# Adding the maximum of a unit's first score buffer directly behind its scores, ahead of the previous unit's last weighted sums

## The chip, the cores and the metric

The kernel is one program on one core of a Trainium2 chip. The metric is the device time of one execution in microseconds (us), the median of several runs; less is better. Work is spread over five engines that each run their own instruction stream and meet at semaphores: TensorE (PE, with its weight loads shown apart as PEld), VectorE (DVE), ScalarE (ACT), GpSimd (POOL), and SyncE (SP), which issues most DMAs.

## The reference

One pre-norm transformer block on 2048 tokens of width 128: an attention layer with 16 heads of 64, and a feed-forward layer whose inputs and weights are rounded to a 4-bit grid in blocks of 16.

```python
qkv = layernorm(x) @ w_qkv                       # 128 -> 3 x 1024
q, k, v = split(qkv), 16 heads of 64
sim = einsum('bhid,bhjd->bhij', q, k) * 64**-0.5
attn = softmax(sim, axis=-1)
x = x + einsum('bhij,bhjd->bhid', attn, v) @ w_out + b_out
xn = layernorm(x)
gate, y = fp4_linear(xn, w_gate), fp4_linear(xn, w_up)   # both sides quantised
x = x + fp4_linear(silu(gate) * y, w_down)
```

Everything is float32. The change touches only the attention: the scores, and the row maximum that the softmax takes off them before the exponential.

## The kernel before, in words

Attention is done in 32 units: 8 pairs of heads, and for each pair 4 blocks of 512 queries. A unit goes through the 2048 keys in 16 steps `j` of 128 keys. The scores stand with keys on the 128 partitions and queries along the free axis, for two heads at a time, in one of two PSUM buffers (`s_ps`, buffer `j % 2`).

On PE, step `j` of a unit (`body`, L1174) issues, in this order:

- for even `j`, one piece of row maxima for the next unit (`row_maxima`, L1155: two matmuls into `mx_ps`, L1016 and L1023; ACT takes the positive part, `rise`, L534, and DVE adds and reduces, L790);
- the scores of step `j + 1` (`scores`, L1000: three products of high and low parts, for two heads, six matmuls), which wait until the exponential has emptied that buffer;
- for odd `j`, the piece of row maxima instead;
- in some steps one piece of other work (`misc`: projections of K, Q, V for coming units, the denominator, the output projection);
- for odd `j`, the weighted sums of steps `j - 1` and `j` (`weighted`, L1151: `probs` times V into `o_ps`), which wait for the exponentials of those steps.

The last step of a unit, `j = 15`, already computes the scores of step 0 of the next unit, into buffer 0.

The maximum itself enters as a matmul too. DVE reduces the pieces to `neg_max` (L798, at step 12), SP copies it by two small DMAs into one row per head, `mrow` (L385), and `maximum` (L1004, matmuls L1008) multiplies a column of ones with that row and adds it to the scores in PSUM. This is done only for the first two steps of a unit (`BACK = 2`). In the remaining steps the keys and values carry what is needed, so `scores` ends the group itself. The exponential of a step (ACT, L614) waits for `s_ready`, which for step 0 is raised by `maximum(0)` and for step 1 by `maximum(1)`.

In the kernel before, `maximum(0)` is the first thing of the unit that it belongs to (L1180 to L1183), so it stands behind the last weighted sums, 14 and 15, of the unit before.

ACT runs in order: exponential of step `j`, at `j = 0` also the copy of the finished `o_ps` of the unit before (`copy_output`, L536 to L540, which waits for all 16 weighted sums of that unit), then the `rise` of one piece of row maxima. POOL adds the exponentials of steps 0 to 12 for the denominator (L497), DVE those of steps 13 to 15 (L913, L918), and POOL adds the two (L503). An exponential also waits until the add that reads its `probs` buffer, four steps back, is done.

The first 24 units run as three turns of a hardware loop of 8 units (L1204); the last 8 are written out, and in them DVE, ACT and POOL already do parts of the feed-forward layer.

Of the kernel before, what the change touches and what calls it, by code (L numbers as in the profile page):

```python
# [51 lines left out]
MAX_LAND = 32  # L52
# [66 lines left out]
def misc_at(w, last):  # L119

    uses = {j: name for j, name in MISC_AT.items() if not skipped(name, w, last)}
    if last:
        uses |= WEIGHTS_AT.get(w, {})
    return dict(sorted(uses.items()))
# [10 lines left out]
def misc_before(it, w, last):  # L135

    return it * (BODY * len(MISC_AT)) + sum(len(misc_at(v, last)) for v in range(w))
# [8 lines left out]
def block_kernel(nc, x_in, w_qkv, w_out, b_out, w_gate, w_up, w_down, out):  # L146
    ctx = ExitStack()
    with ctx:
# [3 lines left out]
        def sem(name):  # L152
            return ctx.enter_context(nc.semaphore(name))
# [110 lines left out]
        s_ready = sem("s_ready")  # L264
# [14 lines left out]
        mrow_landed = sem("mrow_landed")  # L279
# [23 lines left out]
        def at(it, per_unit, w, plus=0):  # L303

            return it * (BODY * per_unit) + (w * per_unit + plus)

        def after(it, per_unit, w, plus=0):

            return at(it, per_unit, w, plus) + START

        def par(w):

            return (w // CHUNKS) % 2
# [203 lines left out]
        def _(act):  # L517
# [79 lines left out]
            def weights_t(name):  # L597

                if name == "down":
                    for i, (_, rows) in enumerate(FF_TILES):  # L600
                        ins = act.activation(wd_t[0:rows, i, :], misc_ps[0:rows, i * DIM:(i + 1) * DIM], ACT.Copy)
                else:
                    at0 = 0 if name == "gate" else FF
                    ins = act.activation(wgu_t[:, at0:at0 + FF], misc_ps[:, 0:FF], ACT.Copy)
                ins.then_inc(misc_free, 1)
# [48 lines left out]
            for what, n in ACT_ORDER:  # L654
                if what == "sign":
                    signs(n)
                elif what == "abs":
                    sizes(n)
                elif what == "T":
                    act.wait_ge(f_xt, n + 1)  # L660
                    act.activation(xq_t[:, n * NX:(n + 1) * NX], banks[4], ACT.Copy).then_inc(f_xt_copied, 1)
                elif what == "silu":
                    act.wait_ge(f_gu, n + 1)
                    if n >= 2:
                        act.wait_ge(f_h, n - 1)
                    act.activation(silu[:, n % 2, :], banks[2 * (n % 2)][:, 0:FF], ACT.Silu).then_inc(f_silu, 1)
                else:
                    act.wait_ge(f_ht, n + 1)
                    if n >= 2:
                        act.wait_ge(f_down, n - 1)  # L670
                    for i, (_, rows) in enumerate(FF_TILES):
                        ins = act.activation(hq_t[0:rows, n % 2, i, :],
                                             banks[5 + n % 2][0:rows, i * P:(i + 1) * P], ACT.Copy)
                    ins.then_inc(f_ht_copied, 1)
# [292 lines left out]
        def _(pe):  # L967
# [25 lines left out]
            def scores(buf, i, q, j):  # L993

                keys = slice(j * P, (j + 1) * P)
                parts = [(k_hi[i][:, keys], q_hi[q]), (k_hi[i][:, keys], q_lo[q]), (k_lo[i][:, keys], q_hi[q])]
                for n, (stationary, moving) in enumerate(parts):
                    for h in range(2):
                        rows = slice(DH * h, DH * (h + 1))
                        ins = pe.matmul(s_ps[:, buf, h, :], stationary[rows, :], moving[rows, :],  # L1000
                                        start=(n == 0 and j < BACK), stop=(n == 2 and j >= BACK), skip_group_check=True)
                return ins

            def maximum(buf):  # L1004

                for h in range(2):
                    rows = slice(DH * h, DH * (h + 1))
                    ins = pe.matmul(s_ps[:, buf, h, :].rearrange("p (t q) -> p t q", t=TQ), ones_r[rows, :],  # L1008
                                    mrow[rows, :].rearrange("p (q t) -> p t q", t=TQ), start=False, stop=True,
                                    skip_group_check=True)  # L1010
                return ins
# [86 lines left out]
            pe.wait_ge(pro_v, CHUNKS)  # L1098
            pe.wait_ge(pro_lo, len(PRO_LO))
            scores(0, 0, 0, 0)  # L1100

            pe.sem_inc(pv_done, P_BUFS)

# [41 lines left out]
            def weighted(it, w, j):  # L1145

                pe.wait_ge(p_ready, after(it, STEPS, w, j + 1))
                if j == 0:
                    pe.wait_ge(o_copied, at(it, 1, w, 1))
                for h in range(2):  # L1150
                    ins = pe.matmul(o_ps[DH * h:DH * (h + 1), :], vv[par(w)][:, j, DH * h:DH * (h + 1)],  # L1151
                                    probs[:, j % P_BUFS, h, :], start=(j == 0), stop=(j == STEPS - 1))
                ins.then_inc(pv_done, 1)

            def row_maxima(it, w, last, j):  # L1155

                u, s = ahead_of(w, j)
                if not runs(last, u, s):
                    return
                final = last and u == BODY  # L1160
                pe.wait_ge(mx_rise, max_no(it, w, j))
                pe.wait_ge(mx_free, max_no(it, w, j))
                if s == 0 and not final:

                    pe.wait_ge(misc_free, misc_no(it, w, "Q", last) + START + 1)
                if s == MAX_STEPS // 2 and w % CHUNKS == CHUNKS - 1 and not skipped("K", w, last):

                    pe.wait_ge(misc_free, misc_no(it, w, "K", last) + START + 1)
                if s == MAX_STEPS // 2 + 1 and w % CHUNKS == CHUNKS - 1 and not skipped("raw", w, last):

                    pe.wait_ge(misc_free, misc_no(it, w, "raw", last) + START + 1)
                max_step(s, par(u), u % Q_BUFS, par(u - 1), (u - 1) % Q_BUFS, final=final)

            def body(it, last):  # L1174
                for w in range(BODY):
                    ahead = not (last and w == BODY - 1)

                    pe.wait_ge(misc_free, misc_before(it, w, last) + START)
                    for j in range(STEPS):
                        if j == 0:  # L1180

                            pe.wait_ge(mrow_landed, at(it, MAX_LAND, w, MAX_LAND))
                            maximum(0).then_inc(s_ready, 1)  # L1183
                        if j % 2 == 0:
                            row_maxima(it, w, last, j)
                        if j < STEPS - 1:
                            pe.wait_ge(p_ready, after(it, STEPS, w, j))
                            ins = scores((j + 1) % 2, par(w), w % Q_BUFS, j + 1)
                            if j + 1 < BACK:
                                ins = maximum(j + 1)  # L1190
                            ins.then_inc(s_ready, 1)
                        elif ahead:
                            pe.wait_ge(p_ready, after(it, STEPS, w, j))
                            scores(0, par(w + 1), (w + 1) % Q_BUFS, 0)
                        if j % 2:
                            row_maxima(it, w, last, j)
                        if j in misc_at(w, last):
                            misc(misc_at(w, last)[j], it, w, last)
                        if j % 2:

                            weighted(it, w, j - 1)
                            weighted(it, w, j)

            with pe.Fori(0, ITERS - 1) as it:  # L1204
                body(it, False)
            body(ITERS - 1, True)
            misc("den", ITERS - 1, BODY, True)

# [68 lines left out]
```

## Time and profile before

| what | value |
|---|---|
| median of 3 runs | 1384.71 us (1379.86, 1384.71, 1384.8) |
| the profiled execution, its own time | 1384.4 us |
| its span, first to last instruction | 1381.5 us |
| mean granted TensorE clock | 0.978 of full |
| PE busy | 1299.0 us (94%) |
| PE weight loads busy | 674.4 us (49%) |
| POOL busy | 1053.9 us (76%) |
| ACT busy | 897.7 us (65%) |
| DVE busy | 798.2 us (58%) |

The span runs from the first to the last instruction; the execution's own time lies 2.9 us above it. Busy time on PE counts overlapping matmuls once, and the ends of matmuls are modelled: the distance from the start of one matmul to the start of the next says more about how PE advances than the duration in the row does. In a row, `x2` behind a matmul means two instructions merged, here the two heads that run side by side. What stands in brackets is the idle time of that engine in front of the instruction and what ended it; "issue" means that the profile shows nothing that the engine waited for.

### The profile page before, as it was taken

The numbers are of one execution on the slowest core, as the hardware profiler recorded it, in microseconds if no ns is written. First come the engines' busy times: TensorE is split into PE (matmuls) and PEld (weight loads), VectorE is DVE, ScalarE is ACT, GpSimd is POOL, SyncE is SP. The second block draws the span as 40 slices with busy tenths as digits, with TensorE's granted clock in tenths as the row PEclk, the third lists the DMA queues.
The fourth block names the chain that finished last, engine by engine and source line by source line (L and its number), as shares of the span: only waits on it lengthen the run. The fifth ranks groups of instructions, "written<-read, shape, count | busy, mean of one in ns | idle before, by whom it ended". The sixth has DMA issues, their size and how long they took to land.

```text
span 1381.5 us, 24376 instructions
## 1 busy us (share of the span) xinstructions
PE 1299.0 (94%) x7541; PEld 674.4 (49%) x7541; DVE 798.2 (58%) x2142; ACT 897.7 (65%) x1300; POOL 1053.9 (76%) x457
## 2 busy tenths in 40 slices
PE   4999999999999999999999999999999999898466
PEld 3555555555455555555445555555555454343245
DVE  6655555555455555555555555555555556777694
ACT  4767666677666766677666676667767667554242
POOL 4488878898778878888788888888988888789232
PEclk9999999999999999999999999999999999999787
DMA  2000000000000000000000000000000000000001
GB/s 61 2 9 2 1 2 9 2 1 1 3 9 2 2 1 9 2 1 1 3 9 2 2 1 9 2 2 1 3 1 1 1 2 1 2 1 1 1 1 30
DMA packets 18300, 6.63 MB, mean 5 GB/s; under 512 B 9696, under 2 KB 18016, under 8 KB 18160
## 3 DMA queue, kind: packets, MB, share of 16 engines
q1 hardware_dynamic: 17936, 4.40, 1.4%
q8 instruction: 66, 1.08, 0.3%
q14 instruction: 74, 0.61, 0.2%
q0 software_dynamic: 224, 0.54, 0.1%
HBM read 3.75 MB, written 1.05 MB: 3 GB/s over the span
## 4 chain that ended last, share of the span: by engine, by line
PE 85%; DVE 7%; issue 4%; POOL 2%; ACT 0%; DMA 0%; POOLq 0%; SPq 0%; DVEq 0%; ACTq 0%
PE o_ps L1151 32%; PE s_ps L1000 24%; PE mx_ps L1023 7%; PE mx_ps L1016 5%; PE misc_ps L1141 3%; PE s_ps L1008 2%; PE misc_ps L1133 2%; PE misc_ps L971 2%; PE misc_ps L983 1%; PE misc_ps L972 1%; PE misc_ps L973 1%; POOL acc_pool L497 1%; PE misc_ps L984 1%; PE misc_ps L985 1%; PE s_ps L1243 1%
## 5 line engine op out<-in xcount | busy, mean ns | idle before, releaser
L497 POOL TENSOR_TENSOR acc_pool<-acc_pool,probs 128x1024 f32<-128x1024 f32 x352 | 853.4, 2424 | 49.5 <-POOL acc_pool L497 40.3
L614 ACT ACTIVATE probs<-s_ps 128x1024 f32<-128x1024 f32 x512 | 527.3, 1030 | 122.1 <-PE s_ps L1008 67.3
L790 DVE CUSTOM_DVE_ANT_0 summed<-mx_ps,rise 128x512 bf16<-128x512 f32 x503 | 344.8, 686 | 424.9 <-issue 354.5
L1151 PE MATMUL o_ps<-probs,vv 128*64 128x512 f32 x2048 | 498.5, 607 | 5.1 <-ACT probs L614 5.1
L534 ACT ACTIVATE rise<-mx_ps 128x512 f32<-128x512 f32 x503 | 301.2, 599 | 271.7 <-PE mx_ps L1016 261.1
L1151 PEld LDWEIGHTS o_ps<-probs,vv 128*64 128x64 f32 x2048 | 127.2, 136 | 229.5 <-issue 174.8
L1016 PE MATMUL mx_ps<-k_raw,q_hi 64*128 64x512 f32 x503 | 224.5, 446 | 10.5 <-DVE part_max L790 9.2
L1023 PE MATMUL mx_ps<-k_hi,q_hi 64*128 64x512 f32 x503 | 224.5, 446 | 1.9 <-DVE part_max L790 1.8
L1000 PE MATMUL s_ps<-q_hi,k_hi 64*128 64x512 f32 x1024 | 207.0, 399 | 0.9 <-ACT probs L614 0.8
L1000 PE MATMUL s_ps<-q_hi,k_lo 64*128 64x512 f32 x1024 | 202.6, 390 | 0.0
L1000 PE MATMUL s_ps<-q_lo,k_hi 64*128 64x512 f32 x1024 | 202.4, 390 | 0.0
L503 POOL TENSOR_TENSOR acc_pool<-acc_pool,acc_dve 128x1024 f32<-128x1024 f32 x32 | 76.2, 2382 | 137.5 <-DVE acc_dve L918 137.5
L1023 PEld LDWEIGHTS mx_ps<-k_hi,q_hi 64*128 64x128 f32 x503 | 92.7, 184 | 179.0 <-issue 178.3
L806 DVE RECIPROCAL rden<-misc_ps 128x128 f32<-128x128 f32 x132 | 120.9, 938 | 13.9 <-PE misc_ps L1133 13.7
L497 POOL TENSOR_TENSOR acc_pool<-probs 128x1024 f32<-128x1024 f32 x32 | 75.9, 2370 | 61.3 <-ACT probs L614 61.3
L1000 PEld LDWEIGHTS s_ps<-q_hi,k_hi 64*128 64x128 f32 x1024 | 98.0, 187 | 38.3 <-ACT probs L614 16.6
L1016 PEld LDWEIGHTS mx_ps<-k_raw,q_hi 64*128 64x128 f32 x503 | 92.7, 184 | 34.7 <-ACT rise L534 15.2
L1000 PEld LDWEIGHTS s_ps<-q_lo,k_hi 64*128 64x128 f32 x1024 | 97.6, 186 | 21.5 <-issue 0.7
L1000 PEld LDWEIGHTS s_ps<-q_hi,k_lo 64*128 64x128 f32 x1024 | 97.0, 185 | 22.4
L814 DVE TENSOR_TENSOR o_norm<-o_raw,rden 128x512 f32<-128x512 f32 x33 | 60.5, 1834 | 0.1
L1008 PE MATMUL s_ps<-mrow,ones_r 64*128 64x512 f32 x128 | 42.6, 661 | 5.4 <-issue 5.4
L777 DVE TENSOR_TENSOR k_lo<-misc_ps,k_hi 128x512 fp32r<-128x512 f32 x28 | 19.4, 692 | 45.5 <-ACT k_hi L520 45.5
(161 smaller groups left out, 1119.0 us busy)
## 6 DMA issues: line engine op xcount, KB each, us to landing
wqkv<-in_L_attn_w_qkv SPq DMA_DIRECT2D x8, 192.0 KB, 3.3
y<-in_L_attn_x SPq DMA_DIRECT2D x4, 256.0 KB, 4.6
mrow<-neg_max SPq DMA_DIRECT2D x64, 2.0 KB, 2.0
out<-y SPq DMA_DIRECT2D x4, 256.0 KB, 2.3
wo<-in_L_attn_w_out SPq DMA_DIRECT2D x8, 64.0 KB, 1.9
wx<-in_L_ffn_w_down POOLq DMA_DIRECT2D x1, 176.0 KB, 6.6
wx<-in_L_ffn_w_gate POOLq DMA_DIRECT2D x1, 128.0 KB, 4.3
wx<-in_L_ffn_w_up POOLq DMA_DIRECT2D x1, 128.0 KB, 4.9
```

The lines of the kernel that those rows point to most:

```text
L497: pool.tensor_tensor(acc, first, probs[:, j % P_BUFS, :, :], ALU.add) \
L503: pool.tensor_tensor(acc, acc, acc_dve[:, w % 2, :, :], ALU.add).then_inc(den_acc, 1)
L534: act.activation(rise[:, h, :], mx_bank(h, pair), ACT.Relu).then_inc(mx_rise, 1)
L614: act.activation(probs[:, j % P_BUFS, :, :], s_ps[:, j % 2, :, :], ACT.Exp, scale=SCALE) \
L790: dve.tensor_tensor_reduce(summed[:, s % 2, :], mx_bank(h, pair), rise[:, h, :], 1.0, LOWEST, ALU.add, ALU.max, part_max[:, slot:slot + 1] ...
L806: ins = dve.reciprocal(rden[:, cols], misc_ps[:, cols])
L814: dve.tensor_tensor(o_norm[:, :], o_raw[:, (w - 1) % 2, :], rden[:, :], ALU.mult).then_inc(o_normed, 1)
L1000: ins = pe.matmul(s_ps[:, buf, h, :], stationary[rows, :], moving[rows, :], start=(n == 0 and j < BACK), stop=(n == 2 and j >= BACK), skip ...
L1008: ins = pe.matmul(s_ps[:, buf, h, :].rearrange("p (t q) -> p t q", t=TQ), ones_r[rows, :], mrow[rows, :].rearrange("p (q t) -> p t q", t=T ...
L1016: return pe.matmul(mx_bank(h, pair), q_hi[q][rows, t * P:(t + 1) * P], k_raw[k][rows, g * QC:(g + 1) * QC], start=True, stop=True)
L1023: return pe.matmul(mx_bank(h, pair).rearrange("p (c n) -> p c n", n=HALF), q_hi[q][rows, t * P:(t + 1) * P], moving, start=True, stop=True)
L1151: ins = pe.matmul(o_ps[DH * h:DH * (h + 1), :], vv[par(w)][:, j, DH * h:DH * (h + 1)], probs[:, j % P_BUFS, h, :], start=(j == 0), stop=(j ...
```

## The change

`maximum(0)` and its wait for `mrow` leave the first step of the unit and go to the end of the last step of the unit before, directly behind the scores that it completes; it counts the landings of one more unit there. For the very first unit it stands directly behind the scores of the prologue. Nothing is added or taken away otherwise: each of the 32 units has one `maximum(0)`, with the same two matmuls.

```diff
             scores(0, 0, 0, 0)
+            pe.wait_ge(mrow_landed, MAX_LAND)
+            maximum(0).then_inc(s_ready, 1)
 
             pe.sem_inc(pv_done, P_BUFS)
...
                     for j in range(STEPS):
-                        if j == 0:
-
-                            pe.wait_ge(mrow_landed, at(it, MAX_LAND, w, MAX_LAND))
-                            maximum(0).then_inc(s_ready, 1)
                         if j % 2 == 0:
                             row_maxima(it, w, last, j)
...
                         elif ahead:
                             pe.wait_ge(p_ready, after(it, STEPS, w, j))
                             scores(0, par(w + 1), (w + 1) % Q_BUFS, 0)
+                            pe.wait_ge(mrow_landed, at(it, MAX_LAND, w, 2 * MAX_LAND))
+                            maximum(0).then_inc(s_ready, 1)
                         if j % 2:
                             row_maxima(it, w, last, j)
```

Only PE's stream changes. At the end of a unit inside the loop, before the change, PE has behind the last two score matmuls (L1000) the row maxima (L1016, L1023), the weighted sums (L1151), and then the maximum (L1008):

```order
L1000 MATMUL s_ps<-q_hi,k_lo 128x512 x2
L1161 REGISTER_ALU
L1016 MATMUL mx_ps<-k_raw,q_hi 128x512 [waits mx_free,mx_rise]
L1023 MATMUL mx_ps<-k_hi,q_hi 128x512
L1151 MATMUL o_ps<-probs,vv 64x512 [waits p_ready]
L1151 MATMUL o_ps<-probs,vv 64x512
L1147 REGISTER_ALU
L1151 MATMUL o_ps<-probs,vv 64x512 [waits p_ready]
L1151 MATMUL o_ps<-probs,vv 64x512
L1178 REGISTER_ALU
L1182 REGISTER_ALU [waits misc_free]
L1008 MATMUL s_ps<-mrow,ones_r 128x512 [waits mrow_landed]
```

The same place in the changed kernel, where lines behind L1100 have moved by up to 4 (the weighted sums are now L1153):

```order
L1000 MATMUL s_ps<-q_hi,k_lo 128x512 x2
L1193 ISA
L1008 MATMUL s_ps<-mrow,ones_r 128x512 [waits mrow_landed]
L1008 MATMUL s_ps<-mrow,ones_r 128x512
L1163 REGISTER_ALU
L1016 MATMUL mx_ps<-k_raw,q_hi 128x512 [waits mx_free,mx_rise]
L1023 MATMUL mx_ps<-k_hi,q_hi 128x512
L1153 MATMUL o_ps<-probs,vv 64x512 [waits p_ready]
L1153 MATMUL o_ps<-probs,vv 64x512
L1149 REGISTER_ALU
L1153 MATMUL o_ps<-probs,vv 64x512 [waits p_ready]
L1153 MATMUL o_ps<-probs,vv 64x512
```

The maximum and its wait for `mrow_landed` have moved ahead of one piece of row maxima and of both weighted sums; the wait for `misc_free` stays at the unit's start.

At the entrance of the loop (L1204), PE's stream as a difference:

```order
 L1000 MATMUL s_ps<-q_hi,k_lo 128x512 x2
+L1008 MATMUL s_ps<-mrow,ones_r 128x512 [waits mrow_landed]
+L1008 MATMUL s_ps<-mrow,ones_r 128x512
 L1204 UNCONDITIONAL_BRANCH
 L1204 ISA
-L1182 ISA [waits misc_free]
-L1008 MATMUL s_ps<-mrow,ones_r 128x512 [waits mrow_landed]
-L1008 MATMUL s_ps<-mrow,ones_r 128x512
-L1161 ISA
-L1023 MATMUL mx_ps<-k_hi,q_hi 128x512 [waits mx_free,mx_rise]
-L1016 MATMUL mx_ps<-k_raw,q_hi 128x512
-L1187 REGISTER_ALU
```

For the first unit the maximum follows its scores in both kernels; only the entrance of the loop now lies behind it. The same holds at the loop's turns: the maximum of the next turn's first unit stands in front of the branch.

## Rows read from the trace of the kernel before

**Rows 1.** The page, part 4: the chain that ended last, by engine.
```profile
PE 85%; DVE 7%; issue 4%; POOL 2%; ACT 0%; DMA 0%; POOLq 0%; SPq 0%; DVEq 0%; ACTq 0%
```
**Rows 2.** Stretches from one maximum to the next: busy (instructions) per engine, PEclk, DMA.
```profile
354.63:393.52 38.89, 38.89 (x229) 20.77 (x229) 20.18 (x59) 26.57 (x37) 29.02 (x13) 0.96 0.04 9
663.28:701.33 38.05, 38.04 (x227) 19.56 (x227) 20.60 (x59) 26.36 (x37) 28.81 (x12) 1.00 0.04 9
701.33:739.42 38.09, 38.07 (x230) 19.41 (x228) 20.77 (x60) 26.37 (x37) 31.22 (x13) 1.00 0.01 1
```
**Rows 3.** Timeline of PE around one unit boundary: start us, us, what.
```profile
698.92 0.39 PE L1000 MATMUL s_ps<-q_hi,k_lo 64*128 64x512 f32 x2
699.15 0.39 PE L1016 MATMUL mx_ps<-k_raw,q_hi 64*128 64x512 f32 x1
...
699.47 1.94 PE L1151 MATMUL o_ps<-probs,vv 128*64 128x512 f32 x8
701.33 0.70 PE L1008 MATMUL s_ps<-mrow,ones_r 64*128 64x512 f32 x2
701.86 0.41 PE L1023 MATMUL mx_ps<-k_hi,q_hi 64*128 64x512 f32 x1
...
702.58 0.39 PE L1000 MATMUL s_ps<-q_hi,k_lo 64*128 64x512 f32 x2
702.81 0.62 PE L1008 MATMUL s_ps<-mrow,ones_r 64*128 64x512 f32 x2
703.25 0.48 PE L1000 MATMUL s_ps<-q_hi,k_hi 64*128 64x512 f32 x2
703.57 0.39 PE L1000 MATMUL s_ps<-q_lo,k_hi 64*128 64x512 f32 x2
...
704.65 0.50 PE L971 MATMUL misc_ps<-dx_hi,wqkv_hi 128*128 128x512 f32 x1
```
**Rows 4.** Timeline of PE's weight loads there, with the wait in front.
```profile
702.58 0.19 PEld L1008 LDWEIGHTS s_ps<-mrow,ones_r 64*128 64x128 f32 x2
703.24 0.18 PEld L1000 LDWEIGHTS s_ps<-q_hi,k_hi 64*128 64x128 f32 x2 [0.46 <-ACT probs L614]
...
704.22 0.18 PEld L1016 LDWEIGHTS mx_ps<-k_raw,q_hi 64*128 64x128 f32 x1 [0.45 <-ACT rise L534]
```
**Rows 5.** Timeline of ACT there.
```profile
699.66 0.59 ACT L534 ACTIVATE rise<-mx_ps 128x512 f32<-128x512 f32 x1
702.16 1.03 ACT L614 ACTIVATE probs<-s_ps 128x1024 f32<-128x1024 f32 x1 [1.91 <-PE s_ps L1008]
703.08 0.59 ACT L540 ACTIVATE o_raw<-o_ps 128x512 f32<-128x512 f32 x1
703.56 0.61 ACT L534 ACTIVATE rise<-mx_ps 128x512 f32<-128x512 f32 x1
```
**Rows 6.** Timeline of POOL there.
```profile
695.29 2.36 POOL L497 TENSOR_TENSOR acc_pool<-acc_pool,probs 128x1024 f32<-128x1024 f32 x1 [0.16 <-POOL acc_pool L497]
701.64 2.38 POOL L503 TENSOR_TENSOR acc_pool<-acc_pool,acc_dve 128x1024 f32<-128x1024 f32 x1 [3.99 <-DVE acc_dve L918]
```
**Rows 7.** SP's issue of the two copies there; landing times of all 64.
```profile
693.60 1.12 SPq L385 DMA_DIRECT2D mrow<-neg_max  x2
...
DMA to landing us min/median/max: 1.9/2.0/3.5
```
**Rows 8.** Timeline of PE at the loop's two turns.
```profile
354.63 0.75 PE L1008 MATMUL s_ps<-mrow,ones_r 64*128 64x512 f32 x2 [2.39 <-issue]
...
663.28 0.71 PE L1008 MATMUL s_ps<-mrow,ones_r 64*128 64x512 f32 x2 [3.06 <-issue]
```
**Rows 9.** Timeline, a boundary among the eight units written out.
```profile
1008.78 0.18 PEld L1016 LDWEIGHTS mx_ps<-k_raw,q_hi 64*128 64x128 f32 x1 [0.44 <-ACT rise L534]
...
1009.21 0.50 PE L971 MATMUL misc_ps<-dx_hi,wqkv_hi 128*128 128x512 f32 x1
```
**Rows 10.** Timeline of PE near the end of the attention.
```profile
1198.95 0.77 PE L1016 MATMUL mx_ps<-k_raw,q_hi 64*128 64x512 f32 x1 [4.63 <-DVE part_max L790]
```

## The prediction, as it was made

> **What bounds the kernel now.** I read the chain that ended last first, then stretches cut from one maximum to the next, then the timeline of each engine around one unit boundary. The chain says that PE carries 85% of the time [rows 1]. The stretches say the same from inside: a unit lasts 38.09 us and PE is busy for 38.07 of them, while ACT is busy for 26.37 and POOL for 31.22 [rows 2]. So only what lets PE's stream advance faster can shorten the time. PE's busy time doesn't show whether that is possible, since a matmul that starts late still overlaps the modelled end of the one before. What shows it is the distance between starts, compared with the distance where nothing is waited for.
>
> At the boundary there is such a loss. PE issues maximum(0) at 701.33, and only that releases the first exponential: ACT had sat idle for 1.91 us before 702.16 [rows 3, 5]. Behind it ACT has the copy of the output (703.08) and the rise (703.56, until 704.17), in order. PE meets both: the weight load of the scores of step 2 starts at 703.24 and names the exponential, which ended at 703.19; the load of the next row maxima starts at 704.22 and names the rise [rows 4, 5].
>
> **What these two waits cost.** From maximum(1) at 702.81 to the K projection at 704.65 PE takes 1.84 us [rows 3]. Without waits I put it together from the same rows: 0.44 behind a maximum (702.81 to 703.25), 0.23 behind each of the three score products (702.58 to 702.81), and 0.32 from row maxima to a matmul of full height (699.15 to 699.47). That is 0.44 + 0.69 + 0.32 = 1.45. The loss is 0.39 us: about 0.09 at 703.57, which comes 0.32 instead of 0.23 behind its neighbour because its weights could not be loaded early, and 0.30 around the row maxima.
>
> **The change part by part.**
>
> *The matmuls themselves.* The same two matmuls are issued, elsewhere. Where they stand now, from the end of the scores to the next row maxima, the path reads 699.15 to 699.47 to 701.33 to 701.86, and the maximum costs 0.53, of which 0.09 is the start behind the weighted sums that whatever stands there pays. Directly behind scores it should cost what maximum(1) costs behind its scores, 0.44. The sum is the same; the bounds are -0.09 and +0.09 a unit. I take 0.
>
> *The first exponential.* Scores of step 0 start their last product at 698.92; maximum(0) then starts at 699.15, and the row maxima follow at 699.59. Their rise, 699.66 now [rows 5], comes at about 700.1. The exponential follows it at about 700.6 instead of 702.16, when the maximum is long done. It also needs POOL's add of step 12, which ended at 697.65, after which POOL idles for 3.99 us [rows 6]. The weighted sums start at 699.91 and end at about 701.85, so the copy starts near 702.0, the rise near 702.5 (the two stand 0.48 apart now) and ends near 703.1. The row maxima that wait for this rise could then start at 703.2, and PE without waits reaches them at 703.25 + 3 x 0.23 = 703.94. Both waits are hidden, the second with 0.7 us to spare, so the whole 0.39 goes. It would come back only if the copy slipped by more than that.
>
> *The order at the tail of the unit.* Row maxima 15 come 0.44 later, and so do DVE's last add and POOL's add of both sums (701.64 becomes about 702.1, until 704.5). POOL's next work needs the exponential of step 1, which ends at about 704.6. Nothing is late; POOL's idle 3.99 grows.
>
> *The added place of a wait.* PE now waits for mrow before the row maxima and the two weighted sums, and everything behind them. The two copies are issued from 693.60 to 694.72 and land after 2.0, at worst 3.5 us, so by 698.22 [rows 7]. PE comes at 699.15 and finds them there. Cost 0; it would begin to cost if a landing took 4.4 us from the end of the issue.
>
> *The loop's turns.* PE stands still for 2.39 and 3.06 us in front of the first maximum of a turn, and waits for nothing shown [rows 8]. That stall stays, in front of the row maxima instead; I take the head's 0.39 there as elsewhere. Behind the first turn the unit runs at clock 0.96 on average and takes 38.89 instead of 38.09; behind the second the clock is 1.00 and the unit takes 38.05 [rows 2]. So a dip to the lower level (1.2 instead of 2.4 GHz) for part of a unit costs 0.8 us and came at one turn of two. I take one again, with -0.8 and +0.8 as bounds. The Trainium skill, "TensorE: Matmul & The Clock Gate", Part 1, says that the clock is halved after a stretch of idleness and that the place of the switch varies from run to run; by that rule a dip at both turns is as allowed as none, and the times would be 1375.0 and 1373.4.
>
> *Counting.* The first unit's maximum follows its scores in both kernels: nothing. Units 2 to 24 run in the loop: 23 x 0.39 = 9.0. The first five written out (25 to 29) show a smaller loss. The row maxima wait for the rise as in the loop (0.44 idle against 0.45), and the next matmul comes 0.43 behind instead of 0.32 [rows 4, 9]; that is 0.30 each, 1.5 together. The last three units are paced by DVE, for which PE waits up to 4.63 us [rows 10]. A PE that is ready earlier waits longer there: 0, with 0 to 0.4 (one maximum that moves into such a wait) on each of the two last boundaries as bounds, 0.8 in all. What was gained earlier is not lost, since DVE's work there depends on matmuls that all come earlier.
>
> Sum: 9.0 + 1.5 = 10.5 us. The profiled execution took 1384.4, 0.3 below the median shown, so the changed kernel takes 1384.4 - 10.5 = 1373.9. With the bounds above (0.8 of the clock, 0.8 at the end, 0.09 x 31 = 2.8 either way for the matmuls' place) the likeliest case spans 1370 to 1378, with half a microsecond or so of noise between runs.
>
> **The rivals.**
>
> *Only the first wait goes.* The copy must wait for the last weighted sum in either order, and the rise stands behind it on ACT. If the copy starts 0.7 us later than I work out, the row maxima wait as before, and only the 0.09 goes: 23 x 0.09 = 2.1, 1382.3. For it speaks that the copy's release is a modelled end. Against it: the copy now starts when its exponential is done, at 703.08, while the sums ended at 699.47 + 1.94 = 701.41 [rows 3, 5]; those 1.7 us are slack. 9%.
>
> *The weights of the maximum are not hidden.* Directly behind the scores, the load of the ones would have to wait for the score matmuls, which use the same rows of the array; 0.19 x 31 = 5.9 comes back and 4.6 is left, 1379.8. Against it speaks that the load of maximum(1) starts at 702.58, with the last score matmuls, and its matmul only 0.23 behind them [rows 3, 4]. The Trainium skill has this rule, "TensorE: Matmul & The Clock Gate", Part 3, The mechanism: a weight load overlaps running matmuls only if it goes to other rows of the array. The trace doesn't agree at maximum(1), and the measurement decides. 4%.
>
> *It was no bound.* Something that I don't see, POOL above all, holds the unit at 38.09 and the boundary's gain returns within the unit. POOL is busy for 31.22 us of it and idles 3.99 in one piece. 1384.4. 7%.
>
> *Slower: the wait for mrow.* If the landing comes after PE reaches its new place, row maxima, both weighted sums and the next unit stand behind it. It decides from 4.4 us after the issue; each further microsecond costs 31 us, and with landings 0.7 us too late the gain of 10.5 turns into a loss of 31 x 0.7 - 10.5 = 11: 1395. Against it: the slowest of 64 landings took 3.5. 3%.
>
> **How the numbers follow.** The forecast gets 77%. A measurement of this kernel tells changes of 0.5% from none, 6.9 us, so faster means below 1377.8. Of the forecast's own range nearly all lies below that (75 of 77). No change takes the rest of it, the first three rivals, and a little of the unknown, 20 in all; slower gets the last rival and some for what I have not thought of, 5. The range reaches up to 1380, over half of the smaller gains, and down to 1369.5, since the runs shown differ by 4.9 us among themselves and the median may fall on their low side.
>
> **What would show it.** Right: a unit in the loop lasts 37.70 us; the first exponential follows the rise without waiting for the maximum, some 1.5 us earlier; the load behind maximum(1) starts under it, and the load of the row maxima names no rise; the distance from maximum(1) to the K projection is 1.45. Wrong: a unit still at 38.0 or more; the loads still naming ACT; PE waiting for mrow at the new place; maximum(0) costing more than 0.5 in front of the row maxima; or the last three units and what follows them growing by what the first 29 gave.

## The result and the profile after

| what | before | after |
|---|---|---|
| median of 8 runs each | 1382.05 us (1379.86 to 1384.8) | 1376.61 us (1373.56 to 1379.18) |
| profiled execution, its own time | 1384.4 us | 1376.88 us |
| its span | 1381.5 us | 1375.3 us |
| mean granted TensorE clock | 0.978 | 0.976 |

The ratio of after to before is 0.9958, 95% interval 0.9943 to 0.9973: the change makes the kernel faster by 0.42%, or 5.8 us of 1382.05 (3.7 to 7.9). The medians themselves differ by 5.4. The forecast was 1373.9 us and a gain of 10.5. The time lies in the stated range, and the direction is the one forecast; the gain is a little over half. The interval leaves out 1, so there is a gain, but by the bound of 0.5% that the prediction set it counts as "no change", with the interval reaching over that bound on its far side. The prediction had written that bound as a time, 1377.8 us, counted from a median of three; 1376.61 lies below that, but from the median of eight the line would be 1375.1.

The boundary first. This is PE's timeline in the changed kernel, at the same boundary as in [rows 3]; columns are start us, us, what.

```profile
694.77 0.40 PE L1000 MATMUL s_ps<-q_hi,k_lo 64*128 64x512 f32 x2
695.01 0.62 PE L1008 MATMUL s_ps<-mrow,ones_r 64*128 64x512 f32 x2
695.45 0.41 PE L1016 MATMUL mx_ps<-k_raw,q_hi 64*128 64x512 f32 x1
...
695.79 1.94 PE L1153 MATMUL o_ps<-probs,vv 128*64 128x512 f32 x8
697.66 0.49 PE L1023 MATMUL mx_ps<-k_hi,q_hi 64*128 64x512 f32 x1
...
698.00 0.40 PE L1000 MATMUL s_ps<-q_hi,k_hi 64*128 64x512 f32 x2
...
698.70 0.62 PE L1008 MATMUL s_ps<-mrow,ones_r 64*128 64x512 f32 x2
699.14 0.42 PE L1000 MATMUL s_ps<-q_hi,k_hi 64*128 64x512 f32 x2
699.39 0.40 PE L1000 MATMUL s_ps<-q_lo,k_hi 64*128 64x512 f32 x2
...
699.86 0.39 PE L1023 MATMUL mx_ps<-k_hi,q_hi 64*128 64x512 f32 x1
...
700.18 0.50 PE L971 MATMUL misc_ps<-dx_hi,wqkv_hi 128*128 128x512 f32 x1
```

The maximum starts 0.24 behind the last score product, whose matmuls start at 694.77, and its weights load at that same time (first row of the weight loads below). It costs 0.44 (695.01 to 695.45). From maximum(1) to the K projection PE now takes 700.18 - 698.70 = 1.48 us, where it took 1.84 [rows 3]. ACT and the weight loads in the same place:

```profile
695.91 0.60 ACT L534 ACTIVATE rise<-mx_ps 128x512 f32<-128x512 f32 x1 [0.29 <-PE mx_ps L1023]
696.40 1.02 ACT L614 ACTIVATE probs<-s_ps 128x1024 f32<-128x1024 f32 x1
697.86 0.60 ACT L540 ACTIVATE o_raw<-o_ps 128x512 f32<-128x512 f32 x1 [0.44 <-PE o_ps L1153]
698.35 0.59 ACT L534 ACTIVATE rise<-mx_ps 128x512 f32<-128x512 f32 x1
699.44 1.03 ACT L614 ACTIVATE probs<-s_ps 128x1024 f32<-128x1024 f32 x1 [0.49 <-PE s_ps L1008]
```

```profile
694.77 0.19 PEld L1008 LDWEIGHTS s_ps<-mrow,ones_r 64*128 64x128 f32 x2
...
698.70 0.19 PEld L1000 LDWEIGHTS s_ps<-q_hi,k_hi 64*128 64x128 f32 x2
699.14 0.21 PEld L1000 LDWEIGHTS s_ps<-q_lo,k_hi 64*128 64x128 f32 x2 [0.25 <-issue]
...
699.63 0.18 PEld L1016 LDWEIGHTS mx_ps<-k_raw,q_hi 64*128 64x128 f32 x1
```

The first exponential (696.40) follows the rise without idle time, 2.30 us ahead of maximum(1); before, it came 0.65 ahead of it [rows 3, 5]. The copy now waits for PE's sums and not for an exponential; the rise ends at 698.94, 0.7 us before its row maxima load their weights. Neither load behind the maximum names ACT any more (compare [rows 4]).

Units, cut as in [rows 2] from one maximum(0) to the next, with the same columns. The second is the third unit of its pair of heads.

```profile
695.01:732.80 37.79, 37.79 (x231) 19.49 (x229) 20.69 (x60) 26.59 (x38) 31.23 (x13) 1.00 0.01 1
732.80:771.01 38.21, 38.10 (x231) 19.53 (x228) 22.95 (x61) 27.09 (x39) 31.38 (x13) 1.00 0.01 1
```

Most units take 37.79 instead of 38.09. Six, one in every four inside the loop, take 38.2, which is more than before. In them DVE is busy for 22.95 us instead of 20.69, and the split that only these units have should account for 0.55 of that. Here is what DVE does there:

```profile
742.92 0.69 DVE L790 CUSTOM_DVE_ANT_0 summed<-mx_ps,rise 128x512 bf16<-128x512 f32 x1 [0.94 <-issue]
...
743.53 2.69 DVE L827 TENSOR_TENSOR wqkv_lo<-wqkv,wqkv_hi 128x384 fp32r<-128x384 f32 x1
746.15 0.68 DVE L790 CUSTOM_DVE_ANT_0 summed<-mx_ps,rise 128x512 bf16<-128x512 f32 x1
```

And POOL, in the changed kernel:

```profile
743.43 2.38 POOL L497 TENSOR_TENSOR acc_pool<-acc_pool,probs 128x1024 f32<-128x1024 f32 x1 [0.16 <-POOL acc_pool L497]
745.97 2.51 POOL L497 TENSOR_TENSOR acc_pool<-acc_pool,probs 128x1024 f32<-128x1024 f32 x1 [0.16 <-POOL acc_pool L497]
```

L827 subtracts the high part from a pair's freshly loaded projection weights, in step 3 of every fourth unit. It started 0.10 us behind a POOL add and ends 0.41 us behind that add's end (745.81), where alone it takes 0.55: all but 0.14 of its work was done after the add. In the kernel before it started 0.06 us ahead of the add, and it was POOL that paid, as DVE's and POOL's rows there show:

```profile
748.26 0.55 DVE L827 TENSOR_TENSOR wqkv_lo<-wqkv,wqkv_hi 128x384 fp32r<-128x384 f32 x1
```

```profile
748.32 2.74 POOL L497 TENSOR_TENSOR acc_pool<-acc_pool,probs 128x1024 f32<-128x1024 f32 x1 [0.16 <-POOL acc_pool L497]
```

The piece of row maxima behind the blocked split (L790 at 746.15) comes late, and PE's next row maxima start at 746.99, 0.28 later than in the unit before, and the matmul behind them another 0.10 later. The profile names no releaser for this wait; in e6 below it names DVE's L790.

The loop's turns, PE's timeline in the changed kernel (before in [rows 8]):

```profile
353.54 0.47 PE L1023 MATMUL mx_ps<-k_hi,q_hi 64*128 64x512 f32 x1 [2.00 <-issue]
...
658.58 0.47 PE L1023 MATMUL mx_ps<-k_hi,q_hi 64*128 64x512 f32 x1 [1.91 <-issue]
```

The stalls were 2.39 and 3.06.

### The profile page after: what moved, and what is told of

Read it like the earlier page. It is cut to its first block, busy times and chain, and to the rows that moved or that the text cites. A ratio compares the mean times of both kernels' runs of the same rounds, so it can differ in the third digit from the quotient of the medians.

```text
span 1375.3 us, 24369 instructions
## 1 busy us (share of the span) xinstructions
PE 1295.0 (94%) x7541; PEld 678.5 (49%) x7541; DVE 805.4 (59%) x2142; ACT 905.1 (66%) x1300; POOL 1053.1 (77%) x457
## 4 chain that ended last, share of the span: by engine, by line
PE 86%; DVE 7%; issue 4%; POOL 2%; ACT 0%; DMA 0%; POOLq 0%; SPq 0%; DVEq 0%; ACTq 0%
PE o_ps L1153 32%; PE s_ps L1000 24%; PE mx_ps L1023 8%; PE mx_ps L1016 4%; PE misc_ps L1143 3%; PE misc_ps L1135 2%; PE s_ps L1008 2%; PE misc_ps L971 2%; PE misc_ps L983 1%; PE misc_ps L972 1%; PE misc_ps L973 1%; POOL acc_pool L497 1%; PE misc_ps L984 1%; PE misc_ps L985 1%; PE s_ps L1243 1%
## 5 line engine op out<-in xcount | busy, mean ns | idle before, releaser
L790 DVE CUSTOM_DVE_ANT_0 summed<-mx_ps,rise 128x512 bf16<-128x512 f32 x503 | 344.8, 686 | 408.9 <-issue 386.9
L1153 PE MATMUL o_ps<-probs,vv 128*64 128x512 f32 x2048 | 498.1, 607 | 5.3 <-ACT probs L614 5.3
L1153 PEld LDWEIGHTS o_ps<-probs,vv 128*64 128x64 f32 x2048 | 127.0, 136 | 237.1 <-issue 174.3
L1016 PE MATMUL mx_ps<-k_raw,q_hi 64*128 64x512 f32 x503 | 225.6, 448 | 10.3 <-DVE part_max L790 8.7
L1023 PE MATMUL mx_ps<-k_hi,q_hi 64*128 64x512 f32 x503 | 225.7, 449 | 6.0 <-issue 3.9
L1000 PE MATMUL s_ps<-q_hi,k_hi 64*128 64x512 f32 x1024 | 205.5, 396 | 0.9 <-ACT probs L614 0.8
L1000 PE MATMUL s_ps<-q_hi,k_lo 64*128 64x512 f32 x1024 | 203.5, 392 | 0.0
L1000 PE MATMUL s_ps<-q_lo,k_hi 64*128 64x512 f32 x1024 | 202.7, 390 | 0.0
L1023 PEld LDWEIGHTS mx_ps<-k_hi,q_hi 64*128 64x128 f32 x503 | 92.8, 184 | 208.4 <-issue 207.2
L1000 PEld LDWEIGHTS s_ps<-q_lo,k_hi 64*128 64x128 f32 x1024 | 98.0, 186 | 28.3 <-issue 7.6
L1000 PEld LDWEIGHTS s_ps<-q_hi,k_lo 64*128 64x128 f32 x1024 | 97.2, 185 | 22.4
L1000 PEld LDWEIGHTS s_ps<-q_hi,k_hi 64*128 64x128 f32 x1024 | 97.6, 186 | 21.1 <-issue 6.5
L1016 PEld LDWEIGHTS mx_ps<-k_raw,q_hi 64*128 64x128 f32 x503 | 92.8, 184 | 26.0 <-issue 13.5
L814 DVE TENSOR_TENSOR o_norm<-o_raw,rden 128x512 f32<-128x512 f32 x33 | 52.8, 1599 | 0.1
L1243 PE MATMUL s_ps<-wgu_t,xq_t 128*128 128x352 f32 x64 | 30.9, 639 | 14.9 <-DVE hh L936 14.1
L1135 PE MATMUL misc_ps<-acc_pool,ones 128*64 128x512 f32 x132 | 36.5, 632 | 8.4 <-POOL acc_pool L503 8.4
```

What stands on the lines that cost most here:

```text
L790: dve.tensor_tensor_reduce(summed[:, s % 2, :], mx_bank(h, pair), rise[:, h, :], 1.0, LOWEST, ALU.add, ALU.max, part_max[:, slot:slot + 1] ...
L814: dve.tensor_tensor(o_norm[:, :], o_raw[:, (w - 1) % 2, :], rden[:, :], ALU.mult).then_inc(o_normed, 1)
L1016: return pe.matmul(mx_bank(h, pair), q_hi[q][rows, t * P:(t + 1) * P], k_raw[k][rows, g * QC:(g + 1) * QC], start=True, stop=True)
L1023: return pe.matmul(mx_bank(h, pair).rearrange("p (c n) -> p c n", n=HALF), q_hi[q][rows, t * P:(t + 1) * P], moving, start=True, stop=True)
L1135: ins = pe.matmul(ps[DH * h:DH * (h + 1), :], ones[:, :], acc_pool[:, (w - 1) % 2, h, :], start=True, stop=True)
```

## The experiments

All were timed beside the kernel before, on one chip for the first four and again for the last three. "Unit" is the distance from one maximum(1) to the next in the loop, from the one profile of each kernel; "every fourth" are the units with the split. Of the eight instances of L827 six stand in the loop, two in what comes before it.

| kernel | ratio to before, 95% | median us | unit | every fourth | L827 us, median of 8 |
|---|---|---|---|---|---|
| before | 1 | 1382.0 | 38.09 | 38.09 | 0.55 |
| e1, the changed kernel again | 0.9958 (0.9944 to 0.9972) | 1375.57 | 37.79 | 38.2 | 2.68 |
| e2, and split at step 13 | 0.9940 (0.9926 to 0.9954) | 1373.73 | 37.79 | 37.79 | 0.56 |
| e3, before, split at 13 | 0.9993 (0.9983 to 1.0003) | 1380.41 | 38.09 | 38.09 | 0.68 |
| e4, before, rise first | 0.9955 (0.9941 to 0.9969) | 1375.65 | 37.81 | 37.91 | 0.55 |
| e5, e2 and maximum behind row maxima | 0.9925 (0.9911 to 0.9939) | 1370.81 | 37.76 | 37.76 | 0.56 |
| e6, before, split at 4 | 1.0035 (1.0020 to 1.0050) | 1387.52 | 38.08 | 38.7 | 2.77 |
| e7, e2 and rise first | 0.9941 (0.9928 to 0.9955) | 1373.26 | 37.79 | 37.79 | 0.56 |

**e1: the changed kernel again.** No edit. Expected:

> The changed kernel once more, as the yardstick beside the others, and to see what its profile repeats. Theory: the change saves 0.30 us a unit at the boundary (38.09 to 37.79 us), and in every fourth unit of the loop (6 units) DVE's split of the weights (L827) starts 0.1 us behind a POOL add instead of 0.06 us ahead of one and waits for it: 2.7 us instead of 0.55, unit 38.2. Then L827 is again 2.7 us in six of eight instances and these units again take 38.2. Rival: that collision is chance of one execution; then L827 differs. The stall at the loop's two turns (2.0 and 2.1 us in the changed kernel's profile, 2.5 and 3.1 in the one of before) and the clock's dip behind one of them vary from run to run. Time 1376 to 1377, 5 to 6 us under before.

The ratio came out the same to the fourth digit, and so did units and split:

```profile
L827 DVE TENSOR_TENSOR wqkv_lo<-wqkv,wqkv_hi x8: 544/2683/2689, 14.9 to 893.1; 128x384 fp32r<-128x384 f32 x8
```

(These are least, middle and longest ns of eight.) The collision is part of the kernel, not an accident of one execution. The stalls at the turns and the clock's dip did vary: this profile has no unit with a clear dip.

**e2: the split moved from step 3 to step 13.**

```diff
-                        if w % CHUNKS == 2 and j == 3 and not last:
+                        if w % CHUNKS == 2 and j == 13 and not last:
                             split_weights(par(w), it * 2 + w // CHUNKS + 3)
```

> The changed kernel with DVE's split of the weights (L827) in the loop moved from step 3 to step 13 of every fourth unit, just ahead of the stretch in which POOL idles 4 us. Theory (the split blocks behind POOL's add at step 3 and delays a piece of row maxima, for which PE waits): the split is at most 1 us, the six units go from 38.2 to 37.8, 6 x 0.4 = 2.4 us less than e1. Rival (those units are slow for another reason, ACT's split of the weights at step 2): they stay at 38.2 and the time is that of e1.

```profile
696.71:734.50 37.79, 37.79 (x230) 19.50 (x228) 20.64 (x60) 26.57 (x38) 31.21 (x14) 1.00 0.01 1
734.50:772.28 37.78, 37.78 (x229) 19.50 (x227) 21.12 (x61) 26.96 (x39) 31.32 (x14) 1.00 0.01 1
```

The unit with the split is now as long as its neighbour, and DVE's busy time is back from 22.95 to 21.12. The median lies 1.8 us under e1, against 2.4 expected. The intervals of the two ratios overlap; the units don't leave a doubt.

The new place is not free of POOL's adds. The split runs between two of them, as DVE's row and then POOL's show:

```profile
764.24 0.56 DVE L827 TENSOR_TENSOR wqkv_lo<-wqkv,wqkv_hi 128x384 fp32r<-128x384 f32 x1
```

```profile
761.99 2.39 POOL L497 TENSOR_TENSOR acc_pool<-acc_pool,probs 128x1024 f32<-128x1024 f32 x1 [0.16 <-POOL acc_pool L497]
764.54 2.48 POOL L497 TENSOR_TENSOR acc_pool<-acc_pool,probs 128x1024 f32<-128x1024 f32 x1 [0.16 <-POOL acc_pool L497]
```

It starts 0.14 ahead of one add's end (764.38) and ends 0.42 behind it, and the next add takes 2.48 instead of 2.38. So e2 takes away the long wait by another phase, and not by a place where POOL idles; that stretch only begins at 767.02.

**e3: the same move in the kernel before.** The edit is that of e2.

> The kernel before with the same move of the split to step 13. In the kernel before the split never collided (0.55 us each), so by the theory this is worth nothing: units stay at 38.09 and the time within 0.5 us of before. Rival (the split at step 3 costs by its place, collision or not): 2 us less than before.

As the theory has it: no change that can be measured (0.9993, interval over 1). The median is 1.6 us below before, not within the 0.5 expected, and the interval reaches down to 0.9983, so the time alone doesn't exclude the rival's 2 us; the units do, at 38.09 all. The split takes 0.68 to 0.70 us at its new place instead of 0.55: it starts 0.26 to 0.28 ahead of a POOL add's end and ends 0.41 to 0.42 behind it, a short block that costs PE nothing.

**e4: only the rise comes earlier.** In the kernel before, on ACT:

```diff
-                        if j == 0:
-                            copy_output(it, w)
...
                         if runs(last, u, s) and not (last and u == BODY):
                             rises(s % 2, max_no(it, w, j))
+                        if j == 0:
+                            copy_output(it, w)
```

> The kernel before, with PE's order untouched; ACT takes the rise of step 0 ahead of the copy of the output. It leaves the wait for the first exponential (0.09 us a unit) and takes 0.48 us off the rise for which PE's next row maxima wait. Theory (of the 0.39 us lost at a boundary 0.30 hang on the rise, and ACT's chain behind the late exponential is what carries it): the rise starts at about 703.1 instead of 703.56, the row maxima are hidden, a unit takes 37.8 us, 29 x 0.28 = 8 us less than before, unless the collision of the split returns in six units (then 6). Rival (the loss is in the exponential alone, or PE waits there for DVE): unit 38.0 to 38.1, time as before.

```profile
700.15 0.19 PEld L1000 LDWEIGHTS s_ps<-q_hi,k_hi 64*128 64x128 f32 x2 [0.46 <-ACT probs L614]
...
700.72 0.18 PEld L1016 LDWEIGHTS mx_ps<-k_raw,q_hi 64*128 64x128 f32 x1
```

The load of the scores still waits for the first exponential, by the same 0.46 as in [rows 4]; the load of the row maxima no longer names the rise. The unit is 0.28 shorter. So of the loss at a boundary the larger part hung on the rise, and one swap on ACT, without any change on PE, gives what the whole change gave (0.9955 and 0.9958). The two totals are made up differently: e4 has 0.28 a unit instead of 0.30, no unit longer than before, and no shorter stall at the turns. The units with the split are at 37.91 here, 0.10 over the others, without a long split. All of the 0.10 is at one matmul ahead of the split, which starts 0.42 instead of 0.32 behind the row maxima before it (744.02). The weights of those row maxima load only at 743.56, 0.12 behind the end of a piece on DVE (L790) that had stood behind DVE's split of K (L777, 742.13 to 742.82). No run tested that.

**e5: the maximum one place later.** On top of e2:

```diff
                             scores(0, par(w + 1), (w + 1) % Q_BUFS, 0)
-                            pe.wait_ge(mrow_landed, at(it, MAX_LAND, w, 2 * MAX_LAND))
-                            maximum(0).then_inc(s_ready, 1)
                         if j % 2:
                             row_maxima(it, w, last, j)
+                        if j == STEPS - 1 and ahead:
+                            pe.wait_ge(mrow_landed, at(it, MAX_LAND, w, 2 * MAX_LAND))
+                            maximum(0).then_inc(s_ready, 1)
```

> e2 with the maximum of step 0 one place later: behind the last piece of row maxima, still ahead of the two weighted sums. The first exponential still comes 1.5 us early, so both waits stay hidden. What differs is whose neighbour the maximum is, and that DVE's and ACT's pieces of the last row maxima come 0.44 us earlier. Theory (the forecast's 0.39 us a unit became 0.30 mostly because the two waits were priced 0.03 too high and the new order of PE costs a few hundredths at its transitions): unit 37.75 to 37.80, time as e2 within 1 us. Rival (delaying the last row maxima by 0.44 is what costs): unit 37.70, 3 us less than e2.

```profile
691.20 0.39 PE L1016 MATMUL mx_ps<-k_raw,q_hi 64*128 64x512 f32 x1
...
691.44 0.62 PE L1008 MATMUL s_ps<-mrow,ones_r 64*128 64x512 f32 x2
691.99 1.94 PE L1153 MATMUL o_ps<-probs,vv 128*64 128x512 f32 x8
```

The unit takes 37.76, 0.03 less and within the expected 37.75 to 37.80, and the rival's 37.70 didn't come. Little of the 0.03 is at the place of the edit: from the last score product to the sums PE takes 1.01 here (690.98 to 691.99) and 1.02 with the maximum in front (694.77 to 695.79). The expected time, within 1 us of e2, was missed. The median is the best of all, 1370.81, some 2.5 us under e7, which ran beside it and is as fast as e2. The profile gives 0.03 x 29 = 0.9 of that. Between the two profiled executions the rest lies in the last three units, a clock dip and a longer stall at one turn of e7; whether it belongs to the edit is open.

**e6: a collision made in the kernel before.** The split at `j == 4` instead of 3, all else as before.

> The kernel before with DVE's split of the weights one step later, at step 4, where by its trace DVE becomes free 0.1 us behind the start of a POOL add. Theory (DVE's operation with two SBUF inputs can't start while POOL's add runs, and PE pays for what DVE then is late): L827 takes 2.3 to 2.7 us in six instances, and the six units go from 38.09 to about 38.5, 2.4 us in all, though the maximum stands where it always stood. Rival (the long L827 is tied to the changed place of the maximum): 0.55 us and 38.09.

DVE and then POOL in this kernel:

```profile
752.67 2.76 DVE L827 TENSOR_TENSOR wqkv_lo<-wqkv,wqkv_hi 128x384 fp32r<-128x384 f32 x1
```

```profile
752.63 2.38 POOL L497 TENSOR_TENSOR acc_pool<-acc_pool,probs 128x1024 f32<-128x1024 f32 x1 [0.16 <-POOL acc_pool L497]
```

And PE, which waits for DVE's late piece:

```profile
758.49 0.46 PE L1016 MATMUL mx_ps<-k_raw,q_hi 64*128 64x512 f32 x1 [0.34 <-DVE part_max L790]
```

The maximum stands where it always stood, and the split is blocked all the same, 0.04 us behind the start of a POOL add. The six units take 38.7, 0.6 more, dearer than the 0.4 expected: 0.50 comes at this row and 0.11 at the matmul behind it. The six add 3.7 us, of the 4.8 that the ratio gives.

**e7: both ways to free the row maxima together.** On top of e2, the edit of e4.

> e2 with, in addition, the rise of step 0 ahead of the copy of the output on ACT, which alone gave 0.28 us a unit in the kernel before. Theory (both edits remove the same wait of PE's row maxima, and PE waits for ACT nowhere else): nothing more to gain, unit 37.79, time as e2 within 1 us. Rival (the two gains are different ones and add up): unit 37.5, 8 us less than e2.

Nothing is added: unit 37.79, ratio 0.9941 against 0.9940 of e2. The two edits remove the same wait.

## Why the prediction was right in kind and too large in size

That the time came within 2.7 us of the forecast is in part luck. The gain was forecast 4.7 us too large, and the time it was taken from was 2.3 us too high; from the median of eight runs the forecast gain would have given 1371.6, 5.1 below what was measured.

*The two waits.* Right in mechanism: both loads stopped naming ACT, the exponential no longer waits for the maximum behind the sums, and e4 and e7 show that the rise carries most of it. The size was too large. The term that was too large is "The loss is 0.39 us": clean, the path from maximum(1) to the K projection takes 1.48 and not 1.45, since a score product behind the maximum's neighbour still comes 0.25 and not 0.23 after it. That makes 0.36.

*The place of the maximum.* I took 0 between -0.09 and +0.09. The maximum itself costs the 0.44 that I gave it, but the sums start 0.34 and no longer 0.32 behind the row maxima, and the scores of step 1 come 0.34 behind theirs, where they came 0.25 before. Against that stand the 0.09 that the maximum no longer pays behind the sums. The orders differ by 0.03. No run isolates this: in e5 the 0.34 behind the sums stays. The 0.33 left against 0.30 measured is within the rounding of some ten distances. Among the units written out, where I forecast 0.30, the profile shows 0.22 (38.01 to 37.79), the same shortfall of 0.08. Over the 28 units of the sum this is 2.5 us too much.

*"Nothing is late".* This is the step that failed outright. I followed every engine to the next thing that it had to meet at the boundary, and not the instruction of every fourth unit that has no partner to meet but shares a resource. Between DVE and POOL the phase of the step decides: 0.06 us ahead of POOL's add the split took 0.55 us, 0.10 behind it 2.68. In six units the gain of 0.30 became a loss of 0.1: 2.4 us. e2, e3 and e6 show it from three sides. In the loop of all nine traces, wherever the split starts with 0.1 us or more of an add still to run, it ends 0.41 to 0.43 behind that add's end, whether 2.4 or 0.1 us were left.

The trace of the kernel before had shown the pair already. DVE's product for the output, L814, has two SBUF inputs too and takes 0.69 us at its shortest, but 1.4 to 2.2 in the loop, here ending 0.55 behind the end (453.39) of the POOL add that ran:

```profile
451.77 2.17 DVE L814 TENSOR_TENSOR o_norm<-o_raw,rden 128x512 f32<-128x512 f32 x1
```

```profile
450.99 2.40 POOL L497 TENSOR_TENSOR acc_pool<-acc_pool,probs 128x1024 f32<-128x1024 f32 x1 [0.16 <-POOL acc_pool L497]
```

Its spread of durations was a sign to look for other such pairs; what these waits cost was not tested. The Trainium skill says of this pair, "SBUF — State Buffer", section "SBUF: two separate sides", that DVE and GpSimd share one pair of ports under an exclusive lock, held by whoever starts first for the whole instruction; a DVE operation with two SBUF inputs takes part in it against a GpSimd operation that reads SBUF. The rows agree, both ways round, but for 0.13 or 0.14 us: the split ends 0.41 behind the add and alone takes 0.55, the add ends 2.25 behind the split (before, 748.81 to 751.06) and alone takes 2.38. That it is this lock is the page's word; the runs show that the two operations all but exclude each other.

*The loop's turns.* I took the stalls as unchanged and the boundary's gain as there. They became shorter. Over the profiles at hand, the sums' last matmul and the next one after the branch lie 2.93 to 3.65 us apart with the maximum behind the branch (before, e3, e4, e6: 8 turns, mean 3.2) and 2.34 to 2.64 with it ahead in nine of ten turns (e7 has one of 3.34; mean of the ten 2.6). The maximum's own 0.44 now runs before the branch; that the engine would have stood still in that time is argued, not shown. Counted from the end of the last exponential of a turn to the first matmul of the next, the two kinds hardly differ (4.0 to 4.7, and 3.9 to 4.2 but for 4.9 at e7's long one), which fits a stall whose end is fixed by something released there. So the turns gave some 1.2 us on average that the sum did not have. What the stall is, the profile doesn't show, and no run took it away.

*The clock.* One dip, as taken. It cost 0.8 before [rows 2] and 1.3 in the changed kernel, where the stretch from the first matmul behind the turn to the same place one unit on took, behind the first turn and the second:

```profile
353.54:391.30 37.76, 37.76 (x229) 19.72 (x229) 20.72 (x59) 26.84 (x38) 29.24 (x13) 1.00 0.04 9
658.58:697.66 39.08, 39.08 (x227) 20.73 (x227) 20.39 (x59) 26.82 (x38) 29.36 (x13) 0.96 0.04 9
```

It came at the other turn than before, and in e1 hardly at all, so it is noise for this comparison.

*The tail.* Right: from maximum(1) of the 30th unit to the end 223.9 us before, 224.3 after. Maximum(0) moved into PE's wait for DVE there and won nothing, as these rows of the changed kernel beside [rows 10] say: PE waits 4.18 instead of 4.63.

```profile
1187.53 0.67 PE L1008 MATMUL s_ps<-mrow,ones_r 64*128 64x512 f32 x2
1192.38 0.76 PE L1016 MATMUL mx_ps<-k_raw,q_hi 64*128 64x512 f32 x1 [4.18 <-DVE part_max L790]
```

*The start.* The profiled execution of before, 1384.4, which the forecast was subtracted from, turned out 2.3 us above the median of eight runs. Against that median the measured gain is 5.8 by the ratio.

*The sum as it should have been.* 17 x 0.30 in the loop, 5 x 0.22 behind it, less 6 x 0.10 for the collisions, and 1.2 at the turns: 5.1 + 1.1 - 0.6 + 1.2 = 6.8 us. The spans of the two profiled executions differ by 6.2, with 0.5 more of clock dip in the changed one; the ratio gives 5.8 with an interval to 7.9.

*Two slips in the sums.* Two dips of the clock or none would have given 1374.7 and 1373.1 from the forecast of 1373.9; the 1375.0 and 1373.4 start from the median of three. And the rest of the forecast's share (2) with the first three rivals (20) makes 22 for no change, not 20. Neither changes the forecast.

*The rivals.* "Only the first wait goes" and "it was no bound" are out by the units at 37.79. "The weights are not hidden" is out by the start of the maximum 0.24 behind the scores. PE waited for mrow at the new place only in the very first unit, where a weight load stands idle for 0.23 us in both kernels. At the boundary shown, SP's two copies were issued from 689.45 to 690.57, over 4 us before the maximum.

## What to carry to other kernels

When a matmul is issued late, its price is not the wait in front of its consumer but what stands behind that consumer in order. Here 0.09 us hung on the exponential and about three times as much on the operation two places further down ACT's queue, and reordering that queue alone was worth as much as moving the matmul. Before trusting a gain of a few tenths in a tightly phased loop, list the operations that exclude one another by resource and not by semaphore, and check which starts first when everything shifts by the gain. An operation of a pair whose duration varies within one trace, as L814's did before the change, points to them. e2 got rid of the long wait by a phase that happens to fit; whether a place where the other engine idles would be safer, no run here tested. And take the base from several runs: here a single profiled execution lay 2.3 us from the median, with an effect of 5.8.

## What the runs showed of the hardware that was not expected

- A subtraction with two SBUF inputs on DVE (128x384) takes 0.55 us if it starts 0.06 us ahead of a POOL add of 128x1024, and 2.68 to 2.79 if it starts 0.01 to 0.11 behind one (after, e1, e6). In the first case the POOL add takes 2.74 instead of 2.38. If it starts 0.13 or 0.14 ahead of an add's end it loses nothing (e2), if 0.26 to 0.28 ahead, 0.12 to 0.14 (e3).
- The operation is shown by the profile as busy for all of that time, so a share of busy time doesn't tell waiting from working: DVE's busy time in the unit with the split was 22.95 us in the changed kernel and 21.12 in e2, for the same work.
- Two matmuls moved from behind a loop's branch to ahead of it shortened the distance across the branch, from the last sums to the next matmul, by 0.6 us on average, where they themselves take 0.44.
